# A recurrent-attention and gated feed-forward layer on one core: eight chunks one by one, or four pairs with seven block products for eight

## The chip, the cores and the metric

The kernel runs on 1 core of one Trainium2 chip. Times are device microseconds of one execution; the kernel before was timed in three runs.

## The reference

The input x is 8 chunks of 512 tokens by 512 features, in float32. Cut to what matters:

```python
xn = layernorm(x)
q, k, v = xn @ Wq.T + bq, xn @ Wk.T + bk, xn @ Wv.T + bv
phi_q, phi_k = elu(q) + 1, elu(k) + 1
kv_sum = cumsum(phi_k * v, over the 512 tokens of a chunk)
s = (phi_q * kv_sum * 32 ** -0.5) @ Wo.T + bo
y = fwht(xn * SU_ug) / 64
up = y @ W_up.T * (Wscale_ug[:2048] * 64)        # 2048 features
gate = y @ W_gate.T * (Wscale_ug[2048:] * 64)
z = fwht(silu(gate) * up * SU_dp) / 64 @ W_down.T * (Wscale_dp * 64)
out = x + s * silu(z)
```

`fwht` is the normalised Walsh-Hadamard transform over the last dimension. The chunks are independent of each other.

## The kernel before

All large products run in float16 on TensorE with float32 sums in PSUM. To keep accuracy each operand is split into a high half and a low half, and a product is three matmuls: high by high, high by low, low by high. A block of 128 output features by 512 tokens over 512 inputs is thus 12 matmuls of 128x128 weights by 512 columns. The transforms are folded into the weights once: butterflies on VectorE across the blocks of 128, and a float32 matmul with a 128x128 Hadamard matrix on TensorE.

All split weights stay in SBUF (`w_attn`, `w_ug`, `w_down`). The first chunk prepares them: SyncE loads them, ScalarE squares them for bounds (`square`, `square_down`, `square_attn`), GpSimd takes maxima over partitions and roots (`weight_max`, `attn_bound`), VectorE derives power-of-two scales (`pow2`), runs the butterflies (`fly_part`, `fly_columns`, `fly_down`, lines 659 and 660), ScalarE takes the high halves out of PSUM (`split_part`, line 384) and VectorE the low ones (lines 697 and 688). Of this the first chunk's products wait.

A chunk then goes so. `transposes` (line 848) turns the normalised x with the identity, ScalarE and VectorE make the high and low halves `xt` (lines 327 and 510). `qkv` makes 12 blocks in a ring of four PSUM banks; ScalarE takes each out with exp and relu or with the bias (`evict_qkv`), VectorE (`attention`, lines 520 to 527) makes the features, the product with v, the scan over tokens and the context. `feed_forward` on TensorE makes 16 times a gate block and an up block (`gate_or_up`, line 836) and one step behind it the down product (`down_product`, line 935) into four further banks. ScalarE takes silu of a gate block (line 405), `hidden` on VectorE multiplies with the up block and splits the result (lines 561 to 568). At the end come `out_product` for the attention's output (line 836 as well, with `w_attn` and `ctx_s`) and `outputs` on VectorE with `silu_outs` on ScalarE. A context is scaled by its maximum over the chunk, which GpSimd brings over the partitions (`ctx_max_of`). The statistics of the next chunk (`ln_stats`, line 491; `normalise`, line 504) lie beside the feed-forward products.

The order of the work is written out by hand for each engine, and semaphores connect them. An instruction that waits holds everything behind it on its engine. SyncE issues all transfers in one queue. Chunks 1 to 6 are a loop; the first and last stand apart.

Of the kernel before, what the change touches and what calls it, by code (L numbers as in the profile page):

```python
# [21 lines left out]
BLOCKS = F // 512  # L42
EPS = 1e-5

X_SCALE = 1024.0
TOP = 14
TINY = 27
TINY_ROOT = 77
TINY_SQUARE = 2.0 ** -100
EXPONENT = 0x7F800000  # L50

# [3 lines left out]

K, V, Q, O = range(4)
SQUARED = (K, Q, O)
M_SU, M_GATE, M_UP, M_DOWN, M_COEF = range(4, 9)
MAXIMA = 9
GATE, UP = 0, 1  # L60

UNITS = [(b, m) for b in range(BLOCKS) for m in (GATE, UP)]
GROUPS = NI // KB
EARLY = 2
AHEAD = EARLY * KB
MARGIN = 1.02
# [3 lines left out]
def build(nc, x, wk_t, wv_t, wq_t, wo_t, gate_t, up_t, down_t, vecs, rows, ident_in, hada_in, out):  # L70
    with ExitStack() as ctx:
        def sb(name, shape, dt=F32):
            return ctx.enter_context(nc.sbuf_tensor(name, shape, dt))

        def sem(name):
            return ctx.enter_context(nc.semaphore(name))


        w_attn = sb("w_attn", [P, 4, 2, KB, D], F16)

        w_ug = sb("w_ug", [P, 2 * BLOCKS * KB * 512])
        w_down = sb("w_down", [P, NI * D])
        ug_raw = w_ug[:, :].rearrange("p (m b k n) -> p m b k n", m=2, b=BLOCKS, k=KB)
        ug = w_ug[:, :].bitcast(F16).rearrange("p (m b k s n) -> p m b k s n", m=2, b=BLOCKS, k=KB, s=2)
        down_raw = w_down[:, :].rearrange("p (k n) -> p k n", k=NI)
        down = w_down[:, :].bitcast(F16).rearrange("p (k s n) -> p k s n", k=NI, s=2)


        x_ln = sb("x_ln", [P, TB, D])
        x_res = sb("x_res", [P, TB, D])  # L90
        xt = sb("xt", [P, 2, KB, T], F16)
        e_k, r_k = sb("e_k", [P, T]), sb("r_k", [P, T])
        e_q, r_q = sb("e_q", [P, T]), sb("r_q", [P, T])
        v_sb = sb("v_sb", [P, T])
        ctx_f = sb("ctx_f", [P, KB, T])
        ctx_s = sb("ctx_s", [P, 2, KB, T], F16)
        scratch = sb("scratch", [P, 4096])
        silu = scratch[:, 0:1024].rearrange("p (r n) -> p r n", r=2)
        gate_g = scratch[:, 1024:2048].rearrange("p (r n) -> p r n", r=2)
# [86 lines left out]
        def flat_attn(m):  # L186
            return raw_attn[m].rearrange("p k n -> p (k n)")
# [130 lines left out]
        def _(act):  # L318
# [110 lines left out]
            for m in (K, V, Q):  # L429
                act.wait_ge(coef_ready, m + 1)  # L430
                split_attn(m)
                if m == K:
                    square_attn(Q)
# [658 lines left out]
```

## Time and profile before

| | |
|---|---|
| time, median of 3 runs | 1460.62 us |
| lowest and highest run | 1457.94, 1460.63 us |
| the profiled execution's span | 1456.1 us |
| its own time | one of the three; 1.8 to 4.5 us above the span |
| PE (TensorE) busy | 1395.5 us |
| DVE (VectorE) busy | 711.4 us |
| ACT (ScalarE) busy | 331.8 us |
| POOL (GpSimd) busy | 25.0 us |
| bytes moved by DMA | 43.04 MB |

The span runs from the first to the last instruction of one execution taken by the hardware profiler. Busy times are sums of instruction durations; matmuls overlap each other, so that TensorE's pace is read from the starts of neighbours in the timeline and not from the duration of one. PEld is the weight load beside the matmuls. In a timeline a row begins with its start and its length, and brackets at the end hold the idle time before it and what ended that. The clock in a windows row is the share of full speed that was granted to TensorE.

### The profile page before, as it was taken

How to read it: one execution, taken by the hardware profiler on the slowest of the kernel's cores; microseconds unless marked ns; L12 is line 12 of the kernel's file. 1: busy time of each engine (PE TensorE's matmuls, PEld its weight loads, DVE VectorE, ACT ScalarE, POOL GpSimd, SP SyncE). 2: the span in 40 equal slices, each digit the busy share in tenths (PEclk: the TensorE clock that was granted, in tenths of full speed). 3: DMA queues.
4: the chain of work that ended last, by engine and by line, in shares of the span. 5: the costliest groups of instructions: out<-in, count | busy, mean ns of one | idle time of the engine just before them, and what ended most of it. 6: DMA issues, size and time to landing. Idle time of an engine off the chain costs nothing.

```text
span 1456.1 us, 16398 instructions
## 1 busy us (share of the span) xinstructions
PE 1395.5 (96%) x6496; PEld 639.5 (44%) x6496; DVE 711.4 (49%) x1143; ACT 331.8 (23%) x454; POOL 25.0 (2%) x35
## 2 busy tenths in 40 slices
PE   1879999999999999999999999999999999999998
PEld 1434344444444444444444444444444444444443
DVE  3879876654236442554326442464326542364324
ACT  3852232230014200140003300141002300142001
POOL 0020000000000000000000000000000000000000
PEclk7889999999999999999999999999999999999999
DMA  9400000200002000100002000110002000010000
GB/s 350 160 0 1 0 29 29 87 1 0 0 6 81 0 0 0 53 33 0 0 0 86 0 0 0 34 53 0 0 0 86 0 0 0 0 58 1 1 0 29
DMA packets 22157, 43.04 MB, mean 30 GB/s; under 512 B 1264, under 2 KB 1520, under 8 KB 22128
## 3 DMA queue, kind: packets, MB, share of 16 engines
q1 hardware_dynamic: 22128, 42.64, 8.2%
q8 instruction: 20, 0.33, 0.1%
q14 instruction: 9, 0.07, 0.0%
HBM read 34.24 MB, written 8.39 MB: 29 GB/s over the span
## 4 chain that ended last, share of the span: by engine, by line
PE 88%; DVE 6%; issue 3%; ACT 1%; POOL 1%; DMA 1%; SPq 0%; DVEq 0%; POOLq 0%
PE ring L836 48%; PE down L935 22%; PE ring L883 5%; PE ring L885 5%; PE ring L884 5%; DVE x_ln L659 1%; DVE x_ln L660 1%; PE ring L848 1%; DVE w_ug L697 1%; PE down L964 1%; DVE w_down L660 1%; PE ring L982 1%; DMA ctx_f<-in_wk_t 1%; POOL norms L301 0%; PE ring L996 0%
## 5 line engine op out<-in xcount | busy, mean ns | idle before, releaser
L836 PE MATMUL ring<-xt,w_ug 128*128 128x512 f16 x3072 | 682.2, 379 | 1.6 <-DVE w_ug L697 1.6
L836 PEld LDWEIGHTS ring<-xt,w_ug 128*128 128x128 f16 x3072 | 300.5, 98 | 366.8 <-DVE w_ug L697 3.2
L561 DVE SCALAR_TENSOR_TENSOR scratch<-ring,up_out,scratch 128x512 f32<-128x512 f32 x128 | 96.1, 751 | 553.9 <-PE ring L836 541.9
L935 PE MATMUL down<-w_down,scratch 128*128 128x512 f16 x1488 | 341.2, 379 | 1.0 <-DVE scratch L568 1.0
L405 ACT ACTIVATE scratch<-ring,gate_out 128x512 f32<-128x512 f32 x128 | 88.0, 687 | 777.2 <-PE ring L836 777.1
L935 PEld LDWEIGHTS down<-w_down,scratch 128*128 128x128 f16 x1488 | 145.5, 98 | 176.3 <-issue 3.2
L883 PE MATMUL ring<-xt,w_attn 128*128 128x512 f16 x384 | 147.6, 384 | 19.4 <-DVE w_attn L647 19.4
L884 PE MATMUL ring<-xt,w_attn 128*128 128x512 f16 x384 | 147.4, 384 | 0.0
L885 PE MATMUL ring<-xt,w_attn 128*128 128x512 f16 x384 | 147.3, 384 | 0.0
L568 DVE TENSOR_TENSOR scratch<-scratch 128x512 f16<-128x512 f32 x124 | 85.9, 693 | 4.3
L836 PE MATMUL ring<-w_attn,ctx_s 128*128 128x512 f16 x384 | 84.2, 379 | 0.0
L883 PEld LDWEIGHTS ring<-xt,w_attn 128*128 128x128 f16 x384 | 37.9, 99 | 64.9 <-issue 21.3
L885 PEld LDWEIGHTS ring<-xt,w_attn 128*128 128x128 f16 x384 | 38.0, 99 | 46.7 <-issue 2.4
L884 PEld LDWEIGHTS ring<-xt,w_attn 128*128 128x128 f16 x384 | 37.9, 99 | 45.2 <-issue 1.7
L836 PEld LDWEIGHTS ring<-w_attn,ctx_s 128*128 128x128 f16 x384 | 37.5, 98 | 45.4
L567 DVE CAST scratch<-scratch 128x512 f16<-128x512 f32 x124 | 52.9, 427 | 4.8
L524 DVE TENSOR_TENSOR_SCAN r_k<-e_k 128x512 f32<-128x512 f32 x32 | 39.2, 1225 | 1.1
L520 DVE SCALAR_TENSOR_TENSOR e_k<-e_k,r_k 128x512 f32<-128x512 f32 x32 | 22.1, 691 | 35.1 <-ACT r_k L375 35.0
L526 DVE SCALAR_TENSOR_TENSOR e_q<-e_q,r_q 128x512 f32<-128x512 f32 x32 | 22.1, 691 | 34.7 <-ACT r_q L375 34.7
L374 ACT ACTIVATE e_q<-ring,vec,i_attn 128x512 f32<-128x512 f32 x32 | 24.9, 778 | 50.6 <-PE ring L885 50.6
L418 ACT ACTIVATE scratch<-scratch 128x512 f32<-128x512 f32 x32 | 20.2, 631 | 67.6 <-DVE scratch L573 67.4
L374 ACT ACTIVATE e_k<-ring,vec,i_attn 128x512 f32<-128x512 f32 x32 | 24.8, 776 | 34.7 <-DVE ctx_f L527 31.4
(123 smaller groups left out, 738.3 us busy)
## 6 DMA issues: line engine op xcount, KB each, us to landing
x_res<-in_x SPq DMA_DIRECT2D x8, 1024.0 KB, 5.3
out<-x_res SPq DMA_DIRECT2D x32, 256.0 KB, 2.0
x_ln<-in_x SPq DMA_DIRECT2D x7, 1024.0 KB, 5.2
w_ug<-in_gate_t SPq DMA_DIRECT2D x4, 1024.0 KB, 14.5
w_ug<-in_up_t SPq DMA_DIRECT2D x4, 1024.0 KB, 14.5
w_down<-in_down_t SPq DMA_DIRECT2D x4, 1024.0 KB, 14.4
x_ln<-in_x SPq DMA_DIRECT2D x4, 256.0 KB, 3.4
ctx_f<-in_wk_t SPq DMA_DIRECT2D x1, 1024.0 KB, 7.6
```

The lines of the kernel that those rows point to most:

```text
L374: act.activation(e[:, :], bank[:, :], ACT.Exp, bias=vec[:, b + f:b + f + 1], scale=unscale)
L405: act.activation(silu[:, i % 2, :], ring[(12 + 2 * i) % 4][:, :], ACT.Silu, scale=gate_out[:, i:i + 1]).then_inc(silu_ready, 1)
L524: dve.tensor_tensor_scan(r_k[:, :], e_k[:, :], e_k[:, :], 0.0, ALU.add, ALU.bypass)
L561: dve.scalar_tensor_tensor(h_f, ring[(13 + 2 * i) % 4][:, :], up_out[:, i:i + 1], silu[:, i % 2, :], ALU.mult, ALU.mult).then_inc(up_read, 1)
L567: chain.after(dve.tensor_copy(h[:, HI, :], h_f))
L568: dve.tensor_tensor(h[:, LO, :], h_f, h[:, HI, :], ALU.subtract).then_inc(h_ready, 1)
L660: return dve.tensor_tensor(d[:, :, 1], a[:, :, 0], a[:, :, 1], ALU.subtract)
L836: mm = pe.matmul(bank[:, :], lhs, rhs, start=(n == 0), stop=(n == len(pairs) - 1))
L883: pe.matmul(ring[n % 4][:, :], w_hi, xt[:, HI, k, :], start=(k == 0), stop=False)
L884: pe.matmul(ring[n % 4][:, :], w_hi, xt[:, LO, k, :], start=False, stop=False)
L885: mm = pe.matmul(ring[n % 4][:, :], w_lo, xt[:, HI, k, :], start=False, stop=(k == KB - 1))
L935: mm = pe.matmul(down_ps[t][:, :], lhs, rhs, start=(i == 0 and n == 0), stop=(i == NI - 1 and n == 2))
```

## The change

The whole program is written anew. What it does:

- Chunks are taken in pairs, and the work of a pair in 22 groups: three for each half of the Q/K/V features (K, V, Q, K, V, Q), then gate and up by turns, eight of each. A group is two row blocks of 128 features (f and its partner in the other half of the features) for both chunks: 2 by 2 tiles of 128x512, over two halves of the 512 inputs.
- In the first pair a group is 4 tiles of 12 matmuls, 8 block products as before. From the second pair on it is 7 block products of 6 matmuls: four weight sums S1 to S4 and four sums T1 to T4 of the transposed x stand beside plain blocks, and each result tile is summed on VectorE from products in PSUM (`add`, 7 for a group). ScalarE copies the first product out (`copy_p1`). Each of the seven products has a bank; it is free when the sum that reads it in this group has been made.
- Split weights no longer stay in SBUF. In the first pair each group's weights are split, used, and stored in DRAM scratch with the split block sums; from the second pair on SyncE loads 1 MB for each group, each quarter of the down weights and the output weights into a ring of five slots, 32 loads a pair.
- The first pair works on weights beside its products: the high and low halves of the next groups, folds for gate and up two groups ahead, the column butterflies and folds of the down weights in four pieces (`first_weights`, groups 4 to 19), and from group 8 on one set of block sums a group (14; the other 8 follow in the down products). GpSimd issues the loads and stores of the block sums.
- The down product of a chunk follows behind all groups of the pair, in quarters; hidden tiles of both chunks stay in SBUF. Transposes of the next pair stand behind the third quarter of the first chunk and the first quarter of the second, and each output product waits for one half of the next x operands.
- Statistics, normalisation and context splitting of a pair lie in the down products, no longer beside gate and up.

The core of the diff, added lines first by table and then by engine:

```diff
+S1, S2, S3, S4, A11, A12, A22 = range(7)
+PRODUCTS = ((A11, B11), (S2, T2), (S3, T3), (S1, T1), (A12, B21), (S4, B22), (A22, T4))
 @block.sync
+            def load_down(e):
+                if e == 0:
+                    sp.wait_ge(attn_squared, 3)
+                else:
+                    sp.wait_ge(d_made, e)
+                sp.dma_start(raw_down(e), down_t[e, :, :, :]).then_inc(d_loaded[e], 16)
+            def store_down(e):
+                sp.wait_ge(d_made, e + 1)
+                for q in range(KB):
+                    dst = scr_d[q, :, :].rearrange("p (a n) -> p a n", n=512)[:, :, e * P:(e + 1) * P]
+                    src = made_down(e)[:, KB * q:KB * q + KB, :, :].rearrange("p k s n -> p (k s) n")
+                    sp.dma_start(dst, src).then_inc(d_stored[e], 16)
...
+            for n in range(GROUPS):
+                if n >= QKV_GROUPS:
+                    store_stage(2 * (n - QKV_GROUPS))
+                    store_stage(2 * (n - QKV_GROUPS) + 1)
+                store_piece(n)
+                if n % 4 == 0 and n >= 8:
+                    if n < 20:
+                        load_down((n - 8) // 4 + 1)
+                    store_down((n - 8) // 4)
...
+            for p in range(1, PAIRS):
+                for n in range(LOADS):
+                    load(p, n)
+                    if n == len(RING) - 1:
+                        store(2 * p - 1)
+                        load_res(2 * p)
+                    if n == GROUPS + 4 and p < PAIRS - 1:
+                        load_x(p + 1)
+                store(2 * p)
+                load_res(2 * p + 1)
 @block.scalar
+            def square_down(e):
+                act.wait_ge(d_loaded[e], 16)
+                if e:
+                    act.wait_ge(d_stored[e - 1], 64)
+                act.activation(fly_down(e).rearrange("p k n -> p (k n)").bitcast(BF16)[:, 0:2048],
+                               raw_down(e).rearrange("p k n -> p (k n)"), ACT.Square,
+                               accum_out=amax[:, M_DOWN + e:M_DOWN + e + 1]).then_inc(d_squared, 1)
...
+                take(0, g, 1)
+                if g % 4 == 0 and 4 <= g < 20:
+                    square_down(g // 4 - 1)
+                if g + 2 >= QKV_GROUPS and g + 2 < GROUPS:
+                    ug_high(g + 2, False)
...
+            def group(p, g):
+                if g:
+                    take(p, g - 1, 2)
+                copy_p1(p, g)
+                if g:
+                    take(p, g - 1, 3)
+                take(p, g, 0)
+                take(p, g, 1)
 @block.vector
+            def add(p, g, step):
...
+                dve.tensor_tensor(tile(g, to), bank[product][:, :], tile(g, other), ALU.add).then_inc(summed, 1)
...
+            def first_weights(g, part):
+                e, step = divmod(g - 4, 4)
+                i, odd = divmod(g - 3, 2)
...
+                if part < 2 and not odd and i < FP:
+                    fly_rows(i, part)
+                if e < KB:
+                    if step == 0 and part == 2:
+                        fly_down_level(e, 0)
+                    elif step == 1 and part == 0:
+                        fly_down_level(e, 1)
+                        scale_down(e)
+                    elif step == 1:
+                        fly_down_level(e, part + 1)
+                    elif step == 2:
+                        take_down(e, part)
...
+                    elif step == 3 and part == 2:
+                        down_low(e)
+                if g >= S_FROM:
+                    if part == 0:
+                        s_sums(g - S_FROM)
+                    elif part == 2:
+                        s_low(g - S_FROM)
...
+            def group(p, g):
+                if g:
+                    add(p, g - 1, 6)
+                    use(p, g - 1, 2)
+                    hidden_low(p, g - 1, 1)
+                add(p, g, 0)
+                if g:
+                    use(p, g - 1, 3)
+                    hidden_low(p, g - 1, 2)
+                add(p, g, 1)
+                if g:
+                    hidden_low(p, g - 1, 3)
+                add(p, g, 2)
+                add(p, g, 3)
+                add(p, g, 4)
+                use(p, g, 0)
+                add(p, g, 5)
+                use(p, g, 1)
+                hidden_low(p, g, 0)
 @block.tensor
+            def fold_down(e, j):
+                if j == 0:
+                    pe.wait_ge(d_flown, e + 1)
...
+            def first_group(g):
+                pe.wait_ge(piece_made, g + 1)
+                e, step = divmod(g - 4, 4)
...
+                for j in range(4):
+                    if 0 <= e < KB and step == 2:
+                        fold_down(e, j)
+                    wait_plain_bank(g, j)
+                    plain_tile(g, j, (0, 1))
+                    if g < 3 and 3 * g + j < FP and j < 3:
+                        norm(3 * g + j)
+                    if QKV_GROUPS <= g + 2 < GROUPS and j in (0, 2):
+                        fold(g + 2, j // 2)
+            def wait_bank(p, g, n):
...
+                elif n == 0:
+                    pe.wait_ge(p1_copied, nth(p, g))
+                else:
+                    pe.wait_ge(summed, 7 * nth(p, g - 1) + (1, 2, 4, 5, 6, 7)[n - 1])
+            def group(p, g):
+                slot = slot_of(p, g)
+                pe.wait_ge(slot_loaded[slot], 16 * loads_into(p, g))
+                if g == 0:
+                    pe.wait_ge(x_ready, 2 * p + 2)
+                for n, (b, c) in enumerate(PRODUCTS):
+                    wait_bank(p, g, n)
+                    terms = [(kk, s, xs) for kk in range(2) for s, xs in ((HI, HI), (HI, LO), (LO, HI))]
+                    for a, (kk, s, xs) in enumerate(terms):
+                        mm = pe.matmul(bank[n][:, :], weight_of(slot, s, b, kk), xops[:, kk, xs, c, :],
+                                       start=(a == 0), stop=(a == 5))
+                    mm.then_inc(product_done, 1)
+            for p in range(PAIRS):
+                for g in range(GROUPS):
+                    if p == 0:
+                        first_group(g)
+                    else:
+                        group(p, g)
+                for a in range(KB):
+                    down_quad(2 * p, a)
+                    if a == 2 and p < PAIRS - 1:
+                        transposes(p + 1, 0)
+                for t in range(TB):
+                    out_product(2 * p, t)
+                for a in range(KB):
+                    down_quad(2 * p + 1, a)
+                    if a == 0 and p < PAIRS - 1:
+                        transposes(p + 1, 1)
+                for t in range(TB):
+                    out_product(2 * p + 1, t)
```

A piece of the down weights that is stored (`store_down`) is 128 by 16 blocks of 128 in a high and a low half, in runs of 128 float16 numbers. `fly_down(e)`, into which `square_down` writes, is the slot that holds the made piece e-1. In group g of the first pair VectorE goes through the parts of `first_weights` behind the use of tiles 0, 1 and 2. `fly_rows` is one of two butterfly levels of 2048 numbers a partition, `fly_down_level` one of four; each is two instructions of 1024.

## Rows read from the trace of the kernel before

**Rows 1.** The page's busy times and the shares of its chain, by engine.

```profile
PE 1395.5 (96%) x6496; PEld 639.5 (44%) x6496; DVE 711.4 (49%) x1143; ACT 331.8 (23%) x454; POOL 25.0 (2%) x35
...
PE 88%; DVE 6%; issue 3%; ACT 1%; POOL 1%; DMA 1%; SPq 0%; DVEq 0%; POOLq 0%
```

**Rows 2.** The waits of PE: us in total, times, longest.

```profile
PE ring L883 <- DVE w_attn L647: 19.4, 1, 19.4
...
PE down L964 <- DVE w_ug L697: 10.9, 1, 10.9
```

**Rows 3.** Windows: from:to, length, busy PE, PEld, DVE, ACT, POOL, PE clock, DMA share, GB/s.

```profile
20.00:30.00 10.00, 0.00 (x0) 0.00 (x0) 2.93 (x9) 2.13 (x4) 0.59 (x1) 0.50 1.05 387
284.00:452.00 168.00, 168.00 (x788) 77.16 (x787) 72.72 (x120) 33.22 (x47) 1.44 (x2) 1.00 0.06 20
```

**Rows 4.** Timeline of PE, end of chunk 0: start us, us, what, count.

```profile
264.93 1.97 PE L848 MATMUL ring<-ident,x_ln 128*128 128x128 f32 x16
266.74 2.75 PE L935 MATMUL down<-w_down,scratch 128*128 128x512 f16 x12
269.33 10.52 PE L836 MATMUL ring<-w_attn,ctx_s 128*128 128x512 f16 x48
279.69 0.38 PE L883 MATMUL ring<-xt,w_attn 128*128 128x512 f16 x1
```

**Rows 5.** Timeline of PE, the first products.

```profile
35.83 0.63 PE L884 MATMUL ring<-xt,w_attn 128*128 128x512 f16 x1
36.26 0.63 PE L885 MATMUL ring<-xt,w_attn 128*128 128x512 f16 x1
```

**Rows 6.** Groups by form on DVE: busy us, mean ns, then idle before and releaser.

```profile
L561 DVE SCALAR_TENSOR_TENSOR scratch<-ring,up_out,scratch 128x512 f32<-128x512 f32 x128 | 96.1, 751 | 553.9 <-PE ring L836 541.9 <-issue 11.6
...
L524 DVE TENSOR_TENSOR_SCAN r_k<-e_k 128x512 f32<-128x512 f32 x32 | 39.2, 1225 | 1.1
...
L520 DVE SCALAR_TENSOR_TENSOR e_k<-e_k,r_k 128x512 f32<-128x512 f32 x32 | 22.1, 691 | 35.1 <-ACT r_k L375 35.0
...
L479 DVE TENSOR_REDUCE ctx_max<-ctx_f 128x1 f32<-128x512 f32 x32 | 21.9, 686 | 1.1
...
L491 DVE BATCH_NORM_STATS2 stats<-x_ln 128x6 f32<-128x512 f32 x32 | 20.0, 682 | 3.3 <-DMA x_ln<-in_x 3.3
L510 DVE TENSOR_TENSOR xt<-ring,xt 128x512 f16<-128x512 f32 x32 | 19.9, 683 | 11.3 <-ACT xt L327 11.3
L504 DVE TENSOR_SCALAR x_ln<-x_ln,mean_var,rstd 128x512 f32<-128x512 f32 x32 | 17.1, 542 | 0.0
```

**Rows 7.** Timeline of DVE, three butterflies; the second waits for the first.

```profile
56.91 1.22 DVE L660 TENSOR_TENSOR x_ln<-w_ug 128x1024 f32<-128x1024 f32 x1
58.16 1.23 DVE L659 TENSOR_TENSOR w_ug<-x_ln 128x1024 f32<-128x1024 f32 x1
59.30 1.22 DVE L660 TENSOR_TENSOR w_ug<-x_ln 128x1024 f32<-128x1024 f32 x1
```

**Rows 8.** Groups by form on ACT.

```profile
L405 ACT ACTIVATE scratch<-ring,gate_out 128x512 f32<-128x512 f32 x128 | 88.0, 687 | 777.2 <-PE ring L836 777.1
...
L327 ACT ACTIVATE xt<-ring 128x512 f16<-128x512 f32 x32 | 16.8, 602 | 36.4 <-PE ring L848 36.4
```

**Rows 9.** The page's DMA packets, and one of its issues with us to landing.

```profile
DMA packets 22157, 43.04 MB, mean 30 GB/s; under 512 B 1264, under 2 KB 1520, under 8 KB 22128
...
x_ln<-in_x SPq DMA_DIRECT2D x7, 1024.0 KB, 5.2
```

**Rows 10.** Timeline, scales and norms: what waited for POOL, in order of time.

```profile
12.46 0.19 ACT L334 ACTIVATION_READ_ACCUMULATOR scratch<-ctx_f 128x1 f32 x1
...
26.93 0.15 DVE L471 TENSOR_SCALAR pw<-amax_all 128x1 f32<-128x1 f32 x1 [11.19 <-POOL amax_all L292]
...
74.12 6.38 POOL L301 TENSOR_TENSOR norms<-norms,half 128x32 f32<-128x32 f32 x1 [25.49 <-DVE norms L731]
...
87.07 0.23 DVE L745 TENSOR_SCALAR pw<-amax_all 128x2 f32<-128x2 f32 x1 [6.35 <-POOL amax_all L282]
```

More of the change, by code:

```diff
@@ L84, in build @@
[L84 to L94, printed above, removed]
@@ new lines, in use, with ctx_absmax @@
+            def use(p, g, j):
+                kind = kind_of(g)
+                if kind == K:
+                    feature(p, g, j)
+                elif kind == V:
+                    times_v(p, g, j)
+                    scan(p, g, j)
+                elif kind == Q:
+                    feature(p, g, j)
+                    context(p, g, j)
+                elif kind == IS_UP:
+                    hidden(p, g, j)
+            def ctx_absmax(p):
+                dve.wait_ge(ctx_made, 8 * p + 8)
+                for n in range(8):
+                    last = absmax(ctx_max[:, n:n + 1], ctx_f(n))
+                prep.after(last)
+                dve.tensor_reduce(ctx_max[:, 8:9], ctx_max[:, 0:8], AX_X, ALU.max).then_inc(ctx_max_ready, 1)
@@ new lines, in _ @@
+            for g in range(GROUPS):
+                first_group(g)
+            o_absmax()
+            use(0, GROUPS - 1, 3)
+            hidden_low(0, GROUPS - 1, 2)
+            hidden_low(0, GROUPS - 1, 3)
+            ctx_absmax(0)
+            s_sums(S_EARLY)
+            o_scale()
+            ctx_scale(0)
+            s_low(S_EARLY)
+            for n in range(4):
+                split_ctx(0, n)
+            o_low()
+            s_sums(S_EARLY + 1)
+            ln_stats(1)
+            s_low(S_EARLY + 1)
@@ new lines, in _ @@
+            normalise(1)
+            s_sums(S_EARLY + 2)
+            for n in range(4, 8):
+                split_ctx(0, n)
+            s_low(S_EARLY + 2)
+            x_sums(1, 0)
+            t_low(1, 0)
+            s_sums(S_EARLY + 3)
+            out_scale()
+            s_low(S_EARLY + 3)
+            outputs(0)
+            s_sums(S_EARLY + 4)
+            s_low(S_EARLY + 4)
+            x_sums(1, 1)
+            t_low(1, 1)
+            for n in range(S_EARLY + 5, GROUPS):
+                s_sums(n)
+                s_low(n)
@@ new lines, in _ @@
+            outputs(1)
+            for p in range(1, PAIRS):
+                for g in range(GROUPS):
+                    group(p, g)
+                last_sums(p)
+                ctx_absmax(p)
+                if p < PAIRS - 1:
+                    ln_stats(p + 1)
+                ctx_scale(p)
+                for n in range(8):
+                    split_ctx(p, n)
+                if p < PAIRS - 1:
+                    normalise(p + 1)
+                    x_sums(p + 1, 0)
+                    t_low(p + 1, 0)
+                out_scale()
+                outputs(2 * p)
+                if p < PAIRS - 1:
+                    x_sums(p + 1, 1)
+                    t_low(p + 1, 1)
+                outputs(2 * p + 1)
```

1758 lines of the change are left out of this document (990 added, 768 removed).

## The prediction

> **What bounds the kernel now.** I read the page's busy times and chain first: TensorE is busy 96% of a span of 1456.1 us and holds 88% of the chain that ended last; VectorE works 49% of it [rows 1]. The list of TensorE's waits is short: 19.4 us for the first split weights and 10.9 us for the fold scale are its largest [rows 2]. The stage view says the rest: one later chunk of 168 us has TensorE busy for all of it at clock 1.00, VectorE for 72.7 us [rows 3]. So only fewer matmuls can help, and VectorE has half its time free to pay for them. The timeline gives the price: 48 matmuls of 512 columns from 269.33 to 279.69 us, 0.2158 us each, and 16 transposes in 1.81 us [rows 4]. A chunk is 768 x 0.2158 + 1.8 = 167.5 us; chunk 0 ends at 279.7 us [rows 4], chunk 1 at 447. Behind the last product 5.7 us remain. After a long wait a matmul takes 0.43 us instead, for some ten matmuls [rows 5]: that costs 2.1 us each time.
>
> The profiled execution's span is 1456.1 us; the median of the runs shown is 4.5 us above it. I sum spans and add the 4.5.
>
> **Pairs 1 to 3: the gain.** Each has 22 groups of 7 products of 6 matmuls (924) and 384 + 96 matmuls of down and output: 1404 x 0.2158 = 303 us, with two sets of transposes 306.6 us, against 335 us for two chunks. That is 28.4 us a pair, 85 us in all.
>
> What TensorE saves, VectorE pays: 7 sums a group from PSUM. The nearest row is the low half of x from PSUM, 0.683 us, of which about 0.62 is its share of the queue; a dependent one is 0.04 longer than its duration [rows 6, 7]. Seven sums: 4.6 us. A gate/up pair of groups adds 4 products (0.65 each) and 4 low halves (0.62): 14.3 us in two groups, where TensorE needs 2 x 42 x 0.2158 = 18.1 us. Covered. In Q/K/V the extra is 2.6 us (K), 7.9 us (V: 0.75 + 1.22 each) and 5.4 us (Q) [rows 6]: 29.7 us against 27.2. Over six groups VectorE falls about 6 us behind. A bank is needed again one group later, which lets it lag 6.5 us. I take 1.5 us of stall a pair. ScalarE has 4 activations of 0.69 us and a copy of 0.60 us in a gate group, 8 and one in a K or Q group, at most 7 of 9.06 us [rows 8]: covered, and if not, the sums wait for the first product's copy.
>
> Weights come from DRAM, 1 MB a group. A 1 MB load lands in 5.2 us [rows 9], and a slot is refilled four groups (36 us) early: nothing. SyncE's queue also holds the stores of a chunk ahead of these loads; it is free again before the next group needs one.
>
> Between pairs TensorE has three quarters of the down product (31.1 us) ahead of the transposes. VectorE has in that time the last hidden tiles (4 us), eight maxima (5.6), the statistics (5.9), a scale (1), eight context splits (10.4) and eight normalisations (3.9): 31 us, with x landing in the middle. I take 2.5 us of stall, twice. Sum: 3 x 303 + 2 x (3.6 + 2.5) + 3 x 1.5 = **925 us**.
>
> **Pair 0: the price.** It makes 8 products as before (1056 matmuls and 7 + 14 us of folds), but all weight work now runs group by group beside it: splits, folds, block sums, stores and reloads, on VectorE and ScalarE, with every queue in a fixed order.
>
> Start to first product: eight x tiles instead of four are normalised, and K lands 3 us later. From K's squares to its scale GpSimd took 14.3 us (12.6 to 26.93), and about 8 us for each next one [rows 10]. K at 30 us; split and low half of x: TensorE starts at **36 us** (35.5 before).
>
> Groups 0 to 5: the squares sit in ScalarE's queue behind Q's scale, which costs TensorE 5 us after group 0. Norms are read at 91 us; the root (6.4 us) and the maximum (6.35 us) on GpSimd [rows 10] give the fold matrix at 107, and TensorE waits from 94: 13 us. Then VectorE is the bound: group 4 holds 14 us for it, group 5 20 us. The first down fold stands ahead of group 6's first tile and waits for the last butterfly: **141 us**.
>
> The same pattern returns at groups 10, 14 and 18; from one to the next four groups pass. TensorE's own work there is 50 us. VectorE's is 53, but unevenly: the group ahead of the fold has hidden 5.1, row butterflies 4.8 and three levels of column butterflies 7.2 (1024 elements, 1.14 or 1.25 us each [rows 7]), splits 1.25, block sums 2.75 and a scale 1.6: 22.7 us beside 11.3 of TensorE. So a cycle is: fold group, cold, 15.6; next group until the down piece is made, 15.8; then ScalarE may not square the next piece before four stores of this one have landed, because it writes into its place. Behind that wait in ScalarE's queue stand the next fold's copy and two gate tiles, and TensorE waits for them. From the landing it is 30 us to the next fold: 3.3 to the copy, 5.1 for a cold tile, 2.6 for the next, and 19 of VectorE's steps. The wait itself is SyncE's issue 0.5, the load ahead of the stores 2.7 (1 MB at 387 GB/s [rows 3]), latency 2 (of 5.2 us for 1 MB [rows 9] 2.5 are not bytes), and X for 4096 packets of 256 B over 16 engines. Cycle: 66.6 + X, the first 65 + X, as block sums begin later.
>
> **X is the number that decides**, and no row has it: this kernel moves only 1264 packets under 512 B of 22157, none of them a bulk load [rows 9]. From below, the bytes at 387 GB/s: 2.7 us. From above, a small packet as slow as one of 2 KB, which takes 16 x 2048 / 387 = 0.085 us: 256 in a row on an engine, 21.7 us. A packet has a fixed part and an eighth of the bytes; I take half the upper end, 11 us, and keep both ends. The Trainium skill speaks against these stores too: its page "DMA: Bandwidth & Descriptors", under Specifications, says that pieces under 512 B are read, modified and written. By the byte rate the sum below would be 1446.5 us, by that rule it is above this by three times what X exceeds 2.7; no run here shows it yet.
>
> Three cycles: 65 + 2 x 66.6 + 33 = 231, to 372. From there 15.6 + 11.3 + 2 x 10.35 = 47.6 us to the last tile, and 2.6 more until the down quarters can be loaded behind the last stores (39.2 + X): **422 us**.
>
> Second half of pair 0: 103.6 us of down and output products. The normalisation for pair 1 ends 40 us in, behind the context maximum's round on GpSimd (6.4), o's split and two block sums; TensorE is ready at 31.1 and waits 9, then runs its transposes cold (+2). Behind the sums of x it waits 2.5 us. With 3.6 of transposes: **121 us**, to 543.
>
> Eight of the 22 block sums are made only here. GpSimd loads their blocks and stores the sums; the trace has no DMA issued by it, so I bound one by SyncE's issue below and one landing (5.2 us) above. The last three sums follow each other without other work, 5 us each, and end some 107 us into this half; their stores and the first 1 MB load of pair 1 land at 116. Five us of cover: nothing, and 5 us if it is gone. VectorE's 2.75 us for each lie beside the down products.
>
> What goes with chunk 0 of before: it took 279.7 us, 112 more than a later chunk, for its own splits and folds. All of that is inside the 447 us against which the 543 stand.
>
> Sum: 422 + 121 + 925 + 5.7 = 1474 us of span, 18 above before, 1478 as a time. About 96 us lost in pair 0 against 80 gained after it. Some 3 us (0.2%) is what a measurement of this kernel can tell from no change.
>
> **Rivals.**
> Faster: the stores go at byte rate, X = 2.7. Place: the three cycles. 3 x 8.3 + 2.6 = 27.5 us less: 1446.5 span, 1451. Break-even is X near 5. For it: only byte rates are seen. Against: packets are eight times smaller than any bulk one in the trace.
> VectorE bounds the seven products: were each sum 0.79 us (0.751 from PSUM and a wait [rows 6]), Q/K/V would ask 5.5 + 5.3 = 10.8 us a group against 9.06, 10.5 us over six groups, of which 6.5 are covered; with refill 6 us a pair, 18 in all: 1496. For: sums depend on each other. Against: the row at 0.683.
> Pair 0 is worse: X = 21.7 adds 3 x 10.7 and as much as 10.7 before the down quarters: 1521.
> It does not save matmuls: only if weights were late; 1 MB per 9.06 us is 116 GB/s of 387. The time would then be over 1500.
>
> **How the numbers follow.** Forecast, X from 6 to 16: 0.45 (1460 to 1498). Byte rate, or shorter stalls in pair 0 than my chain gives: 0.32, of which 0.28 is faster by over 0.2%. VectorE-bound 0.10, the worse pair 0 0.11, late weights 0.02. Slower by over 0.2%: 0.64; within: 0.08. Cases of both signs hold much of the chance; the forecast's own range is 1460 to 1498. The range for 8 in 10 reaches from byte rate with no stall between pairs (1437) to the worst stores (1520).
>
> **What would show it.** Right: 924 matmuls in pairs 1 to 3 at 0.216 us with idle under 3%; pair 0 until about 540 us; TensorE waiting before the fold in groups 6, 10, 14, 18; ScalarE idle on the DMA of the down pieces. Wrong: pair 0 done by 500 us, or stores of 256 B landing in 5 us, or steady TensorE waits on the sums in every group.

## The result, and the profile after

The kernel after takes 1507.0 us (median of four runs, 1505.41 to 1509.34) beside 1459.4 us for the kernel before in the same runs: a ratio of 1.0332, 95% interval 1.0317 to 1.0348. It is 48 us slower, where 18 were forecast. Its profiled execution has a span of 1503.6 us and an own time of 1505.41.

The page of the kernel after, parts 1 to 5; these answer to [rows 1], [rows 9] and, for the sums, [rows 6]:

```profile
PE 1339.2 (89%) x6164; PEld 618.0 (41%) x6164; DVE 1015.2 (68%) x1622; ACT 454.8 (30%) x651; POOL 67.0 (4%) x99
...
PE   1596858867596999999999999999999999999998
...
PEclk8698888879899999999999999999999999999999
...
DMA packets 62797, 201.23 MB, mean 134 GB/s; under 512 B 21888, under 2 KB 22144, under 8 KB 47232
...
L853 DVE TENSOR_TENSOR work<-bank,work 128x512 f32<-128x512 f32 x462 | 305.4, 686 | 91.9 <-PE bank L1399 85.1
```

TensorE has less to do than before, 1339 us for 1395, and yet the span is 47.5 us longer. The strip says where: the last 25 of 40 slices are full, the first 15, pair 0, are not, and the clock there moves between 0.6 and 0.9. The stage view puts numbers to it. Windows of the kernel after, columns as in [rows 3]; the borders are the first product, the folds of the four down pieces (groups 6, 10, 14, 18), the first down product, and the first product of pair 1:

```profile
0.00:39.15 39.15, 5.12 (x33) 4.95 (x34) 14.96 (x40) 12.45 (x16) 3.01 (x9) 0.85 0.96 376
39.15:156.60 117.45, 78.09 (x432) 36.54 (x433) 69.78 (x124) 49.00 (x55) 15.02 (x15) 0.82 0.14 53
156.60:237.90 81.30, 60.41 (x233) 28.75 (x233) 44.13 (x62) 24.75 (x36) 8.41 (x12) 0.85 0.29 94
237.90:320.40 82.50, 60.46 (x232) 28.31 (x232) 51.20 (x74) 27.29 (x40) 13.03 (x20) 0.86 0.37 128
320.40:403.75 83.35, 58.12 (x233) 27.93 (x233) 51.17 (x74) 26.92 (x40) 5.72 (x11) 0.86 0.37 126
403.75:455.80 52.05, 48.83 (x216) 23.13 (x216) 30.25 (x48) 21.58 (x32) 4.26 (x8) 1.00 0.58 206
455.80:575.90 120.10, 109.19 (x513) 50.91 (x514) 86.94 (x154) 23.90 (x28) 12.54 (x19) 0.96 0.57 205
575.90:1503.60 927.70, 918.93 (x4277) 417.53 (x4275) 666.80 (x1052) 268.89 (x404) 4.96 (x5) 1.00 0.35 125
```

| stretch | forecast, us | measured, us |
|---|---|---|
| start to first product | 36 | 39.2 |
| to the fold in group 6 | 105 | 117.5 |
| three cycles, 6 to 18 | 231 | 81.3 + 82.5 + 83.4 = 247.2 |
| group 18 to the first down product | 50 | 52.1 |
| rest of pair 0 | 121 | 120.1 |
| pairs 1 to 3 and what follows | 930.7 | 927.7 |

Two chunks before ended at 447.2 us, pair 0 ends at 575.9: 128.7 us lost. The six other chunks took 1456.1 - 447.2 = 1008.9 us, pairs 1 to 3 take 927.7: 81.2 us gained. The gain is what was forecast; the price is 33 us above it. All of that lies ahead of the down products of pair 0, and in the cycles neither TensorE (60 of 82 us) nor VectorE (44 to 51) is full: a chain of waits sets the time.

The waits of TensorE after, columns as in [rows 2]:

```profile
PE bank L1340 <- ACT gate_g L588: 47.4, 8, 12.9
PE bank L1304 <- DVE xops L802: 23.7, 2, 16.6
...
PE bank L1455 <- DMA ring<-scr_d: 13.1, 2, 10.9
PE bank L1340 <- issue: 12.6, 1, 12.6
PE bank L1399 <- DVE work L853: 2.6, 7, 0.5
```

TensorE waits for folds of gate and up weights that ScalarE copies out of PSUM late (line 588). ScalarE and VectorE are late in turn. Their own waits, us, times, longest, name GpSimd, which the forecast had priced low, and the stores of the down pieces (lines 766 and 1071 are the scales of Q/K/V and of a down piece; line 609 is the square of a down piece):

```profile
DVE pw L766 <- POOL amax_all L460: 31.7, 3, 15.4
DVE pw L1071 <- POOL amax_all L472: 24.1, 3, 8.2
```

```profile
ACT ring L609 <- DMA scr_d<-ring: 11.0, 3, 5.1
```

Behind the 31.7 + 24.1 = 55.8 us of VectorE's waits stands an engine that is busy for 67 us of 1503.6. GpSimd's timeline in the kernel after, start us, us, what, and in brackets the idle time before it; it answers to [rows 10]:

```profile
32.13 0.59 POOL L460 TENSOR_TENSOR amax_all<-amax_all,half 128x1 f32<-128x1 f32 x1 [8.54 <-issue]
40.43 0.38 POOL L456 PARTITION_ALL_REDUCE amax_all<-amax  x1 [7.71 <-issue]
48.41 0.59 POOL L460 TENSOR_TENSOR amax_all<-amax_all,half 128x1 f32<-128x1 f32 x1 [7.61 <-issue]
55.34 0.38 POOL L456 PARTITION_ALL_REDUCE amax_all<-amax  x1 [6.34 <-issue]
63.41 0.59 POOL L460 TENSOR_TENSOR amax_all<-amax_all,half 128x1 f32<-128x1 f32 x1 [7.70 <-issue]
...
214.98 1.03 POOL L456 PARTITION_ALL_REDUCE amax_all<-amax  x1 [7.03 <-issue]
223.36 0.27 POOL L471 TENSOR_SCALAR amax_all<-amax_all 128x1 f32<-128x1 f32 x1 [7.35 <-issue]
223.71 0.60 POOL L472 TENSOR_TENSOR amax_all<-amax_all,half 128x1 f32<-128x1 f32 x1
```

A partition maximum (PARTITION_ALL_REDUCE) takes 0.38 us and a root (line 460 or 472) 0.59 us, but ahead of each the engine stands 5.9 to 8.5 us with no wait that the profile shows, wherever the one kind follows the other (the shortest is 5.85 us, ahead of the maximum at 120.14 us). Between 223.36 and 223.71, two arithmetic instructions in a row, the second of which waits for the first by a semaphore too, there is nothing: the semaphore is not the cost. A maximum with its root thus costs 15 to 16 us, and K, V and Q come at 32.7, 49.0 and 64.0 us.

GpSimd in the kernel before already stood still in the same places. This part of its timeline is not in [rows 10]:

```profile
26.31 0.59 POOL L292 TENSOR_TENSOR amax_all<-amax_all,half 128x1 f32<-128x1 f32 x1 [8.26 <-issue]
33.33 0.38 POOL L282 PARTITION_ALL_REDUCE amax_all<-amax  x1 [6.44 <-issue]
33.63 0.42 POOL L289 PARTITION_ALL_REDUCE amax_all<-amax  x1
41.22 0.59 POOL L292 TENSOR_TENSOR amax_all<-amax_all,half 128x1 f32<-128x1 f32 x1 [7.17 <-issue]
```

From one root's end to the next it took 14.9 us there, 26.9 to 41.8. The Trainium skill, page "GPSIMD Engine Reference", section "Instruction dispatch", says that the first call to a freshly loaded kernel of this engine pays about 6 us that no instruction shows. The rows show such an unseen time, 5.9 to 8.5 us, at each change and not once only; whether it is a load of code, no run here shows.

The stores of a down piece, over which the forecast was most in doubt, in the kernel after:

```profile
188.80 0.33 SPq L321 DMA_DIRECT2D ring<-in_down_t  x1
189.18 6.62 SPq L328 DMA_DIRECT2D scr_d<-ring  x4
...
270.63 0.33 SPq L321 DMA_DIRECT2D ring<-in_down_t  x1
...
353.53 0.33 SPq L321 DMA_DIRECT2D ring<-in_down_t  x1
```

```profile
199.52 1.91 ACT L609 ACTIVATE ring<-ring 128x2048 bf16<-128x2048 f32 x1 [4.38 <-DMA scr_d<-ring]
...
282.71 1.91 ACT L609 ACTIVATE ring<-ring 128x2048 bf16<-128x2048 f32 x1 [1.54 <-DMA scr_d<-ring]
...
366.11 1.91 ACT L609 ACTIVATE ring<-ring 128x2048 bf16<-128x2048 f32 x1 [5.11 <-DMA scr_d<-ring]
```

SyncE asks for the next piece as soon as one is made. The first piece is made at 188.8 and has landed at 199.5: 10.7 us. The next two take 12.1 and 12.6. The forecast had 5.2 of that without X. If these 5.2 are right, X is 5.5, 6.9 and 7.4 us, for the 11 taken; a run below tests them.

### The profile page after: what moved, and what is told of

Read it like the earlier page. It is cut to its first block and busy times, and to the rows that moved or that the text cites. A ratio compares the mean times of both kernels' runs of the same rounds, so it can differ in the third digit from the quotient of the medians.

```text
span 1503.6 us, 16253 instructions
## 1 busy us (share of the span) xinstructions
PE 1339.2 (89%) x6164; PEld 618.0 (41%) x6164; DVE 1015.2 (68%) x1622; ACT 454.8 (30%) x651; POOL 67.0 (4%) x99
## 5 line engine op out<-in xcount | busy, mean ns | idle before, releaser
L1399 PE MATMUL bank<-xops,ring 128*128 128x512 f16 x2772 | 601.1, 379 | 2.9 <-DVE work L853 2.6
L1399 PEld LDWEIGHTS bank<-xops,ring 128*128 128x128 f16 x2772 | 269.8, 98 | 333.7 <-DVE work L853 10.9
L853 DVE TENSOR_TENSOR work<-bank,work 128x512 f32<-128x512 f32 x462 | 305.4, 686 | 91.9 <-PE bank L1399 85.1
L1455 PE MATMUL bank<-ring,h_all 128*128 128x512 f16 x1536 | 335.9, 380 | 13.1 <-DMA ring<-scr_d 13.1
L1304 PE MATMUL bank<-xops,ring 128*128 128x512 f16 x1056 | 256.2, 402 | 23.7 <-DVE xops L802 23.7
L1455 PEld LDWEIGHTS bank<-ring,h_all 128*128 128x128 f16 x1536 | 150.6, 98 | 194.9 <-DMA ring<-scr_d 14.1
L1304 PEld LDWEIGHTS bank<-xops,ring 128*128 128x128 f16 x1056 | 108.3, 103 | 168.3 <-issue 55.9
L662 ACT ACTIVATE h_all<-work 128x512 f16<-128x512 f32 x128 | 80.7, 630 | 320.2 <-DVE work L892 320.2
L1340 PE MATMUL bank<-h_all,hsu 128*128 128x256 f32 x128 | 40.4, 445 | 73.3 <-ACT gate_g L588 47.4
L901 DVE TENSOR_TENSOR h_all<-work,h_all 128x512 f16<-128x512 f32 x128 | 87.7, 685 | 0.4
L1481 PE MATMUL bank<-ring,ctx 128*128 128x512 f16 x384 | 84.2, 379 | 0.0
L655 ACT ACTIVATE work<-work,gate_out 128x512 f32<-128x512 f32 x96 | 66.4, 715 | 54.4 <-DVE work L853 54.4
L892 DVE SCALAR_TENSOR_TENSOR work<-work,up_out 128x512 f32<-128x512 f32 x96 | 71.3, 743 | 0.0
L642 ACT ACTIVATE work<-work,vec,i_attn 128x512 f32<-128x512 f32 x48 | 38.8, 809 | 75.2 <-DVE work L853 75.2
L874 DVE TENSOR_TENSOR_SCAN work<-work 128x512 f32<-128x512 f32 x32 | 39.2, 1224 | 1.1
```

Of the source, the lines that this page charges most:

```text
L655: act.activation(tile(g, j), src, ACT.Silu, scale=gate_out[:, at:at + 1]).then_inc(act_tiles, 1)
L662: act.activation(h[:, i, TILE_OF[j], HI, :], tile(g, j), ACT.Copy).then_inc(h_hi, 1)
L853: dve.tensor_tensor(tile(g, to), bank[product][:, :], tile(g, other), ALU.add).then_inc(summed, 1)
L874: dve.tensor_tensor_scan(tile(g, j), tile(g, j), tile(g, j), 0.0, ALU.add, ALU.bypass) \
L892: dve.scalar_tensor_tensor(tile(g, j), src, up_out[:, at:at + 1], tile(g - 1, j), ALU.mult, ALU.mult).then_inc(h_made, 1)
L901: dve.tensor_tensor(at[:, LO, :], tile(g, j), at[:, HI, :], ALU.subtract).then_inc(h_ready, 1)
```

## The experiments

Two theories. **A**: the excess is the changes between maximum and root on GpSimd. **B**: it is the stores of the down pieces and the wait behind them on ScalarE, or elsewhere. The kernels come from the one after by the edits shown.

**Root of a down piece's bound on VectorE.** A power of two goes into the scale anyway, so the root's exponent is halved in its bits, and the factor 1.4143 covers what that leaves out.

```diff
 @block.gpsimd
-                chain.after(all_max(M_DOWN + e, M_DOWN + e + 1))
-                at = amax_all[:, M_DOWN + e:M_DOWN + e + 1]
-                chain.after(pool.tensor_scalar(at, at, MARGIN, TINY_SQUARE, ALU.mult, ALU.max))
-                pool.tensor_tensor(at, at, half[:, 0:1], ALU.pow).then_inc(d_bounded, 1)
+                all_max(M_DOWN + e, M_DOWN + e + 1).then_inc(d_bounded, 1)
...
 @block.vector
+            def root_bits(at):
+                prep.after(dve.tensor_scalar(at.bitcast(I32), at.bitcast(I32), EXPONENT, None, ALU.bitwise_and))
+                prep.after(dve.tensor_scalar(at.bitcast(I32), at.bitcast(I32), 0.5, float(127 << 22),
+                                             ALU.mult, ALU.add))
...
+                prep.after(dve.tensor_scalar(mx, mx, MARGIN, TINY_SQUARE, ALU.mult, ALU.max))
+                root_bits(mx)
```

> Edit: GpSimd only takes the maximum over partitions for a down piece; the factor, the floor and the root move to VectorE as three instructions of 0.15 to 0.2 us (the root by halving the exponent bits). Theory A (my price for a maximum followed by a root on GpSimd, 8 us, was half of what it costs: 17 us from the store of the sums to the result, because the two kinds of work by turns cost about 7 us each): VectorE's 24.1 us of waits for the root go, each of the three cycles from 81 to 83 us becomes 73 to 75 us, the whole 20 to 25 us shorter, 1482 to 1487. Theory B (the cycle is set by the landing of the down stores, and the root lies beside that): at most 5 us shorter, 1502 or more.

Measured: 1487.0 us, 20.0 less; ratio to before 1.0183 (1.0165 to 1.0201). The cycles are 74.3, 75.6 and 75.2 us. GpSimd in this kernel:

```profile
208.75 0.58 POOL L489 DMA_DIRECT2D scr_g<-ring  x1 [9.86 <-DVE ring L984]
209.36 0.31 POOL L457 PARTITION_ALL_REDUCE amax_all<-amax  x1
```

The maximum now follows a DMA issue without a gap, where 7.03 us stood before: the gap belongs to the change from arithmetic, not to the maximum. VectorE's wait for the down bounds is gone from the list, and of TensorE's wait for the folds that ScalarE copies out late, 47.4 us in the kernel after, a good half is left:

```profile
PE bank L1347 <- ACT gate_g L586: 25.2, 8, 5.2
```

Theory A, at the lower edge of the gain that it named.

**Root of the Q/K/V bounds on VectorE.**

```diff
 @block.gpsimd
-                root_max(m).then_inc(attn_bounded, 1)
+                all_max(m, m + 1).then_inc(attn_bounded, 1)
...
 @block.vector
-                pow2(amax_all[:, m:m + 1], MARGIN, ...
+                root_bits(amax_all[:, m:m + 1])
+                pow2(amax_all[:, m:m + 1], ROOT2 * MARGIN, ...
```

> Edit: the roots of the bounds of K, V and Q leave GpSimd as well, to VectorE; the maxima over partitions stay. Theory A (roots between maxima make each of the three take 15 to 16 us): K's scale comes 6 to 8 us earlier, V's and Q's within a few us of it and of their data; TensorE's first product at about 33 us in place of 39.2, its waits of 7.2 and 5.6 us in groups 0 and 1 go; group 6 begins at 135 to 142 us in place of 156.6, the whole 15 to 21 us shorter, 1486 to 1492. Theory B (the squares in ScalarE's queue and the transposes set the start): less than 6 us shorter.

Measured: 1482.8 us, 24.2 less; ratio 1.0149 (1.0132 to 1.0166). In GpSimd's timeline the three maxima stand in one row, and TensorE's first product comes 9.3 us earlier:

```profile
22.66 1.05 POOL L457 PARTITION_ALL_REDUCE amax_all<-amax  x3 [9.60 <-issue]
```

```profile
29.84 12.10 PE L1308 MATMUL bank<-xops,ring 128*128 128x512 f16 x48 [6.22 <-DVE xops L805]
```

Group 6 folds at 133.55 instead of 156.6 us: 23 us, of which 9.3 lie ahead of the first product and 14 in Q's, V's and the squares' wait behind them. Theory A, and by more than it said.

**Square of a down piece into free space.** ScalarE no longer waits for the stores; VectorE's first butterfly does.

```diff
 @block.scalar
-                if e:
-                    act.wait_ge(d_stored[e - 1], 64)
...
+                unkept = work[:, 12:14, :] ... if e else fly_down(e) ...
+                if e:
+                    act.wait_ge(d_squared, e)
...
 @block.vector
                 if level == 0:
                     dve.wait_ge(d_squared, e + 1)
+                    if e:
+                        dve.wait_ge(d_stored[e - 1], 64)
```

> Edit: the unused output of the squares of down pieces 1 to 3 goes to two exp tiles that are idle by then; ScalarE no longer waits for the down stores, VectorE waits for them ahead of the first butterfly instead. Theory B (ScalarE's wait, 11.0 us in all, holds the next fold's copy and with it TensorE, which then also goes cold): 4 to 5 us less a cycle, 12 to 15 in all, 1492 to 1495. Theory A (the root on GpSimd is what ends last in each cycle, and what ScalarE gains is waited away there): the waits on GpSimd grow from 24.1 us by what ScalarE's lose, and the time falls by less than 6 us.

Measured: 1496.1 us, 10.9 less; ratio 1.0244 (1.0227 to 1.0261). ScalarE's 11.0 us of wait are gone, and VectorE waits longer for GpSimd's root:

```profile
DVE pw L1075 <- POOL amax_all L472: 31.6, 3, 11.2
```

The total is between what the two theories gave. Of what came free, 7.5 us went into the next wait in the chain, 24.1 to 31.6, and still 10.9 came out: the 11.0 us on ScalarE had held up more than themselves, perhaps through the two tiles in its queue behind them. So both theories hold a share, and this run by itself does not part them.

**Third and fourth down quarters loaded ahead of the output weights.** Before the third quarter TensorE had waited 10.9 us; the load stood in SyncE's queue behind the wait for the split output weights (`o_made`):

```diff
             load_x(1)
+            load_first_quad(2)
+            load_first_quad(3)
             sp.wait_ge(o_made, 1)
...
-            for n in range(2, 2 * KB - 1):
+            for n in range(4, 2 * KB - 1):
```

> Edit: in SyncE's queue the loads of the third and fourth down quarter stand ahead of the wait for the split output weights. TensorE waited 10.9 us for the third quarter in the down product of chunk 0, which I had not foreseen; I had 9 us of wait in the same place for the normalised x. Theory A (x comes at 491.2 us, 4 us after TensorE would have been ready, and the sums of x cannot begin before the context splits end at 499.7): the 10.9 us wait goes, one of about 4 us for x takes its place and one for the x operands grows, the whole only 2 to 4 us shorter. Theory B (the slot was the only brake): 9 to 11 us shorter.

Measured: 1507.5 us, 0.5 more; ratio 1.0314 (1.0295 to 1.0333), no difference from the kernel after. TensorE in the kernel after, and then in this one:

```profile
487.61 12.42 PE L1455 MATMUL bank<-ring,h_all 128*128 128x512 f16 x48 [10.88 <-DMA ring<-scr_d]
```

```profile
496.64 2.95 PE L1418 MATMUL bank<-ident,work 128*128 128x128 f32 x16 [4.37 <-DVE work L797]
...
515.59 4.85 PE L1483 MATMUL bank<-ring,ctx 128*128 128x512 f16 x11 [4.95 <-DVE xops L834]
```

The largest wait of this half, once removed, comes back as 4.37 us for the normalised x, transposes that run slow behind it, and 4.95 us for the operands of the output product. VectorE's chain to the next x was just as late, and the half takes 121.3 us for 120.1. Neither theory had the time unchanged; the first, with 2 to 4 us of gain, was the nearer.

**Stores in runs of 2 KB.** On top of the first experiment, a piece is stored in one run for each partition and quarter. The down weights then lie in scratch in another order, so the down product multiplies other weights than the reference's, with the same work in the same places.

```diff
-                    dst = scr_d[q, :, :].rearrange("p (a n) -> p a n", n=512)[:, :, e * P:(e + 1) * P]
-                    src = made_down(e)[:, KB * q:KB * q + KB, :, :].rearrange("p k s n -> p (k s) n")
+                    dst = scr_d[q, :, e * 1024:(e + 1) * 1024]
+                    src = made_down(e)[:, KB * q:KB * q + KB, :, :].rearrange("p k s n -> p (k s n)")
```

> Edit: e1_down_root, and each quarter of a down piece is stored in one run of 2 KB a partition instead of eight of 256 B; the down weights then lie in another order in DRAM, so the down product uses them in a wrong order (same sizes and counts). Compared with e1_down_root (1487.0 us). My X was taken at 11 us; in the profile after the stores land 10.7 us after the piece is made, which by my own sum is X = 5.5. If 256 B pieces cost twice their bytes' time, the landing comes 2.5 to 3 us sooner, ScalarE's wait for it (9.3 us in three) falls under 2 us and the time by 5 to 9 us, to 1478 to 1482. If the pieces cost nothing extra (the load ahead of them and the latency are the wait), it stays within 2 us.

Measured: 1486.8 us for 1487.0 with the first edit alone; ratio 1.0186 (1.0168 to 1.0204) for 1.0183, no difference. SyncE and ScalarE in the first experiment, and then here:

```profile
190.65 6.67 SPq L329 DMA_DIRECT2D scr_d<-ring  x4
...
200.90 1.91 ACT L607 ACTIVATE ring<-ring 128x2048 bf16<-128x2048 f32 x1 [4.29 <-DMA scr_d<-ring]
```

```profile
190.53 2.45 SPq L329 DMA_DIRECT2D scr_d<-ring  x4
...
199.67 1.91 ACT L607 ACTIVATE ring<-ring 128x2048 bf16<-128x2048 f32 x1 [3.17 <-DMA scr_d<-ring]
```

SyncE issues the four stores in 4.2 us less, but from the start of the issue to the landing it takes 9.1 us for 10.3. For the next two pieces it is 11.2 for 11.6, and 11.0 for 12.0. That is all that pieces of 256 B cost here: 0.3 to 1.1 us. ScalarE's wait for the landings, us, times, longest, did not shrink in sum. In the first experiment, and then here:

```profile
ACT ring L607 <- DMA scr_d<-ring: 9.3, 3, 4.3
```

```profile
ACT ring L607 <- DMA scr_d<-ring: 11.1, 3, 4.1
```

So the 5.2 us that the forecast had without X were too few. With the bytes at 2.7 us it had 7.9 us from a piece made to a piece landed in runs of 2 KB; here it takes 9.5, 11.6 and 11.4. An estimate from the two: X itself is 3.0 to 3.8 us (2.7 and the 0.3 to 1.1), and the load ahead, the issue and the latency take the rest. Which of these was short, no run parts.

**The first four edits, and the norms' root on VectorE too**, with the maximum of the norms taken at once:

```diff
 @block.gpsimd
-            pool.wait_ge(norms_read, 1)
-            pool.tensor_tensor(norms[:, :], norms[:, :], half[:, :], ALU.pow).then_inc(norms_ready, 1)
 @block.vector
-                dve.wait_ge(norms_ready, 1)
+                dve.wait_ge(norms_read, 1)
+                root_bits(norms[:, :])
+                prep.after(dve.tensor_scalar(norms[:, :], norms[:, :], ROOT2, None, ALU.mult))
...
                         read_norms()
+                        norms_max()
                         fly_rows(0, 0)
                         fly_rows(0, 1)
-                        norms_max()
```

> Edit: the four edits together, and the roots of the norms on VectorE too, with their maximum taken at once. Theory A (each change of GpSimd between a maximum over partitions and arithmetic costs 7 to 8 us, a maximum alone 0.3 us): the norms' root (6.4) and the change behind it (6) go as well, 10 to 12 us; with the 20, 24 and 11 us measured singly the sum is 1507 - 66 = 1441, 1435 to 1447: faster than the kernel before. Rival (the single gains overlap, the in-order queues of VectorE and ScalarE take back half): 1460 or more.

Measured: 1436.1 us, ratio 0.9837 (0.9821 to 0.9854): 23 us faster than before, 71 less than after, as theory A had it. The single gains add to 20.0 + 24.2 + 10.9 = 55.1; the wait for the fold matrix fell from 12.6 to 5.3 us, 7.3 more. The remaining 8 us are not assigned; two waits in series that each hid part of the other would give that, which is not shown.

**Row butterflies one group earlier.** In the odd groups from 5 on `fly_rows` stood beside three levels of column butterflies of a down piece or its low halves; now it stands in the even groups, where VectorE has less.

```diff
-                i, odd = divmod(g - 3, 2)
+                i, odd = divmod(g - 2, 2)
```

> Edit: e6_all, and the row butterflies of a pair of groups move one group earlier, from the up groups into the gate groups (i from g - 2 in place of g - 3), so that VectorE's 53 us of a cycle lie as about 12, 12, 11 and 18 in place of 7, 16, 7 and 23. Theory (TensorE waits ahead of groups 6, 10, 14, 18 for the group in which VectorE has 23 us beside 11): each cycle 4 to 5 us shorter, group 6 too, 13 to 20 us in all against e6_all. Rival (ScalarE's chain through the fold copies sets the cycle): less than 5 us.

Measured: 1422.1 us, 14.1 less than the last; ratio 0.9745 (0.9729 to 0.9761). The load on VectorE, group by group, held this back, as the forecast's "unevenly" had it.

**Norms read at the end of group 2**, one group earlier, on top of it:

```diff
-                    elif part == 2 and g == 3:
+                    elif part == 2 and g == 2:
                         read_norms()
                         norms_max()
+                    elif part == 2 and g == 3:
                         fly_rows(0, 0)
```

> Edit: e7_balance, and the norms are read and their maximum asked for at the end of group 2 in place of group 3. Theory: TensorE's wait for the fold matrix in group 4 (12.7 us before these edits) has 7 us or less left, the whole 2 to 6 us less than e7_balance. Rival: VectorE is behind there anyway, and the time stays within 2 us.

Measured: 1421.2 us, 0.8 less than the last and within the spread of runs; ratio 0.9744 (0.9728 to 0.9760). The wait for the fold matrix went from 5.3 to 4.3 us only. The rival was right. This is the best version: 38 us faster than the kernel before, 86 than the one after. TensorE's waits in it:

```profile
PE bank L1427 <- DVE work L797: 21.1, 3, 17.4
PE bank L1351 <- ACT gate_g L582: 13.1, 6, 2.8
```

The wait for ScalarE's tiles has fallen from 47.4 to 13.1 us; the first transposes (17.4 us, before anything else can start) are now the largest.

**The kernel before, with its roots on VectorE.** It shows how much of that lead the roots alone would give the kernel before. The roots of K, Q and the output weights, of the norms and of the down weights move as above (V has none there), and the norms' maximum is asked for ahead of a butterfly.

```diff
-                pool.wait_ge(pool_step, n)
-                pool.tensor_tensor(amax_all[:, m:m + 1], amax_all[:, m:m + 1], half[:, 0:1], ALU.pow) \
...
-            pool.tensor_tensor(norms[:, :], norms[:, :], half[:, :], ALU.pow).then_inc(norms_ready, 1)
...
-            pool.tensor_tensor(amax_all[:, M_DOWN:M_DOWN + 1], amax_all[:, M_DOWN:M_DOWN + 1], half[:, 0:1],
-                               ALU.pow).then_inc(down_bounded, 1)
...
 @block.vector
-                part(1, UP)
...
+                root_bits(norms[:, :])
...
+                part(1, UP)
```

> Edit: the kernel before, with the roots of K, Q, O, the norms and the down bound moved from GpSimd to VectorE in the same way, and the norms' maximum asked for ahead of a butterfly. If a change between kinds of work on GpSimd costs 7 to 8 us wherever it stands, K's scale comes some 8 us earlier and the fold scale 10 us or more: TensorE's waits of 19.4 and 10.9 us shrink to about 11 and under 2, the whole 13 to 20 us shorter, 1440 to 1446. Rival: those stages are bound by loads and by VectorE, and the time stays above 1453. Either way it says how much of e8_norms's lead (1421.2 against 1458.9) is the seven products' and how much the roots'.

Measured: 1437.5 us, 21.0 less than before; ratio 0.9855 (0.9839 to 0.9872). That is a little more than the 13 to 20 us named. The two waits of [rows 2] have become:

```profile
PE ring L888 <- DVE w_attn L649: 7.8, 1, 7.8
PE down L969 <- DVE w_ug L699: 3.3, 1, 3.3
```

So the kernel before had paid the same cost. With it gone from both, the pairs with seven products are ahead by 1437.5 - 1421.2 = 16.3 us. That lead is not the seven products' alone: the version of 1421.2 us has the edits of order and balance as well, which the kernel before was not given.

## Why the forecast was wrong

The direction held. The size did not, 48 us for 18: 1507.0 us lies above the forecast's own 1460 to 1498, and only within its 8 in 10 (1437 to 1520). The place of the loss, pair 0, was right; the reason given for it was not the one that made it.

**Pairs 1 to 3: right.** 927.7 us for 925 + 5.7. The seven sums take 0.686 us each, as the row of 0.683 said, and TensorE waits for them 2.6 us in 462 sums. The rival in which VectorE bounds them is refuted, as are late weights.

**The step that failed** is, under start to first product, "about 8 us for each next one". From 14.3 us between K's squares and its scale [rows 10] I took 8 us for a maximum and root that follow another, which no row of [rows 10] shows; the rows after show 15 to 16 (32.7, 49.0, 64.0), since the engine changes kind twice, and the trace of before had 14.9. For the down bounds no price for the root was in the chain at all. The rows of before held the hint too: 6.35 us of wait for a maximum was taken as its own time [rows 10], which is 0.37 us in that trace. What it measured: 24.2 us for Q/K/V, where my sum held about 11 (first product 36 for 29.8, and 5 behind group 0), and 20.0 us for the down pieces, where it held nothing. That is 33 us too little.

**X, "the number that decides": the second mis-sized term.** From a piece made to a piece landed I had 16.2 us, 11 of them X; it took 10.7, 12.1 and 12.6. By my own other terms X is 5.5, 6.9 and 7.4 us. The run with stores of 2 KB puts it lower, at 3.0 to 3.8 by the estimate above, and shows that the other terms were too small by 1.6 to 3.7: two errors that in part hid each other. With the whole way as measured and all else unchanged my sum would have been 1474 - (5.5 + 4.1 + 3.6) - 2.6 = 1458 us, 2 above before (the 2.6 stood for the last stores outlasting the last tiles); X at 11 made the forecast look nearer than it was. The rule of the Trainium skill's page "DMA: Bandwidth & Descriptors", section "Specifications", on pieces under 512 B did not bear on the time with any weight: pieces of 256 B cost 0.3 to 1.1 us of landing for 1 MB, and nothing in the total.

**From landing to the next fold**, forecast at 30 us, took 38.4 (199.52 to 237.89). With the root moved it takes 31.4 (200.90 to 232.33): that chain was right but for the same term. The part ahead of the first landing took 42.9 us for 35 + 5.5.

**First product, group 6.** 39.2 for 36 and 117.5 for 105: the roots again, as group 6 at 133.6 us without them shows. The wait for the fold matrix was 12.6 us for 13.

**Second half of pair 0: right in size, not in the cause named.** 120.1 for 121. I had TensorE wait 9 us for x; it waited 10.9 us for a down quarter, whose load stood behind a waiting store on SyncE, and the run that removed this gave nothing, because x was as late.

**Rivals.** Byte rate, 1451, was the furthest off in time. VectorE as the bound (1496), the worse pair 0 (1521) and late weights (over 1500) came near the time by luck: pairs 1 to 3 took what the forecast gave them, which refutes the first and the last, and pair 0 was worse by another mechanism than slower stores. What was missing among them is GpSimd as the bound, and I had passed it over because it is busy for 2% of the span [rows 1].

The account: some 45 us lie between 1458, the sum with the landings as measured, and the span of 1503.6. The roots are 33 of it. Another 7.5 lie in the cycles even without the roots: 225.1 us in the first experiment, where my chain with its landings (10.6, 12.0 and 12.4 us from a piece made) gives 217.6. The last 5 us are not assigned.

## What to carry to other kernels

Read an engine's busy time and its idle time that ends in no wait as two things: a nearly idle GpSimd held the chain here, because maxima over partitions and arithmetic alternated on it. Keep one kind of work there, in a row, and move a root to where its consumer runs. A wait that is removed is worth only what the next one in the chain lets through: of 10.9 us at one place nothing came out, and 11 us at another gave 10.9 while the wait behind it grew by 7.5.

## What the runs showed that was not expected

- A change between a partition maximum and arithmetic on GpSimd costs 5.9 to 8.5 us each time, in either direction; a DMA issue behind either of them costs nothing of that kind. Three maxima in a row take 1.05 us in all.
- 1 MB stored to DRAM in 4096 pieces of 256 B lands 0.3 to 1.1 us later than in runs of 2 KB, though SyncE's issue of four such stores takes 6.7 us for 2.45 (the first piece).
- TensorE's granted clock was 0.82 to 0.86 in the stretches of pair 0 where it kept waiting, and 1.00 from pair 1 on, where it was busy for 99% of the time. In the best version the mean over the span rose from 0.954 to 0.976 as waits went.
